# One barrier fewer, two steps earlier and a fed matrix engine at the joints of a graph network

## The reference

```
h = jnp.maximum(_layernorm(x, axis=-1), 0.0)
...
h = _gat_conv(x, src, dst, W1, att_src1, att_dst1, b1, N)
h = _leaky(_graph_norm(h, gn_weight, gn_bias, gn_mean_scale), NEG_SLOPE_ACT)
h = _gat_conv(h, src, dst, W2, att_src2, att_dst2, b2, N)
h = _graph_norm(h, gn_weight, gn_bias, gn_mean_scale)
return _leaky(h + residual, NEG_SLOPE_ACT)
...
out = jax.ops.segment_sum(x[col] * norm[:, None], row, num_segments=num_nodes)
```

## Time and profile before

| what | us |
| --- | --- |
| median of 3 runs (lowest, highest) | 862.6 (862.21, 863.18) |
| the profiled execution's own time | 864.48 |
| its span, from first to last instruction | 862.7 |
| mean granted clock of PE | 0.921 of full |
| PE busy, DVE busy, ACT busy | 747.3, 629.5, 478.8 |

### The profile page before, as it was taken

One profiled execution on the slowest core, in us unless ns is written; L12 is line 12 of the kernel. 1 busy time (PEld: TensorE's weight loads), 2 busy tenths in 40 slices (PEclk: granted clock), 3 DMA queues, 4 the chain that ended last, 5 costly groups with the idle time before them and its releaser, 6 DMA issues. The chain is left out here.

```text
span 862.7 us, 21079 instructions
## 1 busy us (share of the span) xinstructions
PE 747.3 (87%) x8209; PEld 680.8 (79%) x8209; DVE 629.5 (73%) x1696; ACT 478.8 (56%) x911; POOL 4.3 (0%) x14
## 2 busy tenths in 40 slices
PE   7898889887997998999997589988854999887898
PEld 6666656657996998999997578888753988876797
DVE  7899999985455544433444789998878999987732
ACT  2698889881004122122224588888665988874600
POOL 1000000000000000000000000000000000000000
PEclk9799999997997999999999579999955999998899
DMA  4000000005990000000002100000001489776901
GB/s 136 12 12 12 12 4 2 2 2 177 415 382 1 2 2 1 2 2 2 13 13 93 31 2 17 17 17 2 1 1 33 96 178 195 158 150 156 189 24 34
DMA packets 98735, 56.02 MB, mean 65 GB/s; under 512 B 91160, under 2 KB 93130, under 8 KB 98504
## 3 DMA queue, kind: packets, MB, share of 16 engines
q1 hardware_dynamic: 98292, 53.78, 23.0%
q10 hardware_dynamic: 340, 0.84, 0.3%
HBM read 9.16 MB, written 24.97 MB: 40 GB/s over the span
## 5 line engine op out<-in xcount | busy, mean ns | idle before, releaser
L631 PE MATMUL banks<-y_sb,adjacency 128*128 128x192 f16 (+1 forms) x1875 | 167.1, 250 | 6.0 <-DVE y_sb L668 5.2
L631 PEld LDWEIGHTS banks<-y_sb,adjacency 128*128 128x128 f16 x1875 | 162.6, 99 | 7.0 <-DVE y_sb L668 5.3
L469 PEld LDWEIGHTS counts<-hot_code,hot_row 128*128 128x128 f16 x1568 | 96.5, 103 | 59.9 <-DVE hot_code L352 35.4
L469 PE MATMUL counts<-hot_code,hot_row 128*128 128x100 f16 (+3 forms) x1568 | 124.8, 223 | 20.1 <-DVE hot_code L352 15.3
L1761 PE MATMUL banks<-loose,y_sb 128*128 128x194 f16 x540 | 101.4, 251 | 0.0
L352 DVE TENSOR_TENSOR hot_code<-codes_iota,unpacked 128x600 f16<-128x600 f16 x196 | 97.2, 563 | 0.0
L1760 PE MATMUL banks<-x_sb,gat_masks 128*128 128x194 f16 x420 | 79.8, 252 | 16.6 <-DVE gat_masks L1684 8.2
L572 ACT ACTIVATE adjacency<-counts 128x800 f16<-128x800 f32 x98 | 81.6, 833 | 21.5 <-PE counts L469 21.3
L1760 PE MATMUL banks<-x_sb,y_sb 128*128 128x194 f16 x400 | 75.0, 250 | 13.9 <-DVE h_sb L1684 9.9
L1731 ACT ACTIVATE gat_masks<-y_sb,node_scalars 128x640 bf16<-128x640 f32 x84 | 67.9, 825 | 23.1 <-PE banks L1761 17.9
L1760 PE MATMUL banks<-x_sb,h_sb 128*128 128x194 f16 x430 | 75.8, 247 | 0.8
(11 more groups left out here) (244 smaller groups left out, 1353.3 us busy)
## 6 DMA issues: line engine op xcount, KB each, us to landing
kept_adj<-adjacency SPq DMA_DIRECT2D x5, 4000.0 KB, 32.1
y_sb<-a_dst_rows SPq DMA_DIRECT2D x10, 320.0 KB, 3.5
window_keys<-edge_keys SPq DMA_DIRECT2D x188, 5.0 KB
residual<-h_sb SPq DMA_DIRECT2D x5, 240.0 KB, 2.0
kept_x<-x_sb SPq DMA_DIRECT2D x1, 1200.0 KB, 4.5
loose<-residual SPq DMA_DIRECT2D x5, 240.0 KB, 3.4
x_sb<-kept_x SPq DMA_DIRECT2D x5, 240.0 KB, 4.8
x_sb<-in_x SPq DMA_DIRECT2D x4, 240.0 KB
```

The source lines that it names most:

```text
L469: last = nc.tensor.matmul(counts[:, 2 * (p % HELD) + i, start:end], hot_row[:, q % 2, b * QUAD + w, :], hot_codes(q % 2, b)[:, w, start - ...
L631: return nc.tensor.matmul(k.ps[:, j % G, 0:cols], k.ADJ[:, i, j * P:(j + 1) * P], y[:, i, 0:cols], start=i == 0, stop=i == NT - 1)
```

## The change

Five edits. (1) The clearing of semaphores and the second meeting of all engines behind attention 1 are gone; a list of semaphores that are older than attention 1, without the two of `row_ready`, is cleared by POOL as its first instruction inside attention 1. (2) In both attentions piece 2 is measured ahead of the last five adds instead of behind `write`. (3) In graph_norm bn_aggr is issued ahead of three short instructions instead of behind them. (4) In `last_norm` `low(g - 1)` goes ahead of the lift in each round, and lifts 3 and 4 are both done in round 1. (5) In place of 48 idle-time matmuls in a row there are 83, in ten pieces, each behind a wait for a step of group 0 on DVE or ACT.

```diff
-def clear_semaphores(nc, k):
-    nc.clear_and_free_semaphores(k.held)
-    nc.all_engine_barrier()
-    k.held = []
...
+            measure(nc, k, dve, t.tiles_turned, t.measured, MEASURED_EARLY)
             for q in range(G):
                 add(NG - 1, q)
             write(NG - 1)
-            for n in range(MEASURED_EARLY, NC + 1):
+            for n in range(MEASURED_EARLY + 1, NC + 1):
                 measure(nc, k, dve, t.tiles_turned, t.measured, n)
...
         @block.gpsimd
         def _(pool):
+            if passed:
+                nc.clear_and_free_semaphores(passed)
...
+        chain.later(dve.bn_aggr(k.columns[:, 4:6], k.column_stats.rearrange("p n e -> p (n e)")))
         chain.later(dve.tensor_scalar(unit, k.mscale, -1.0, None, ALU.mult))
         chain(dve.tensor_scalar(less, k.mscale, -1.0, 1.0, ALU.mult, ALU.add))
-        chain.later(dve.tensor_tensor(less, less, k.gat_bias, ALU.mult))
-        chain(dve.bn_aggr(k.columns[:, 4:6], k.column_stats.rearrange("p n e -> p (n e)")))
+        chain(dve.tensor_tensor(less, less, k.gat_bias, ALU.mult))
...
             moments(g)
-            if g + 2 < NG:
-                lift(g + 2)
             if g >= 1:
                 low(g - 1)
+            for later in {0: (2,), 1: (3, 4)}.get(g, ()):
+                lift(later)
             scales(g)
...
-        keep_busy(sums(0)[:, 0:P], FILL_MORE)
+        for step, count, times in ((s.added, 1, 10), (s.measured, G, 14), (s.row_moments, G, 16), (s.row_shift, 1, 10)):
+            pe.wait_ge(step, count)
+            keep_busy(sums(0)[:, 0:P], times)
+        for t in range(G):
+            pe.wait_ge(s.normal, t + 1)
+            keep_busy(sums(0)[:, 0:P], 5)
+        pe.wait_ge(s.high, 1)
+        keep_busy(sums(0)[:, 0:P], 8)
         over_chunk(0, 0, AT_ONCE)
...
-        attend(nc, k, d, "gat1", d.gat_b1)
-        clear_semaphores(nc, k)
+        passed = [s for s in k.held if s not in k.row_ready]
+        attend(nc, k, d, "gat1", d.gat_b1, False, passed)
```

More of the change, by code:

```diff
@@ L1418, in turn_chunk, with attend @@
                      d.kept_adj[a * G * P:(a + 1) * G * P, m * G * P:(m + 1) * G * P], transpose=True).then_inc(k.adj_turned[m], 16)
-def attend(nc, k, d, name, b, last=False):
+def attend(nc, k, d, name, b, last=False, passed=()):
     with ExitStack() as c:
@@ L1880 @@
 LEAK = 0.01
-FILL, FILL_MORE = 32, 48
+FILL = 32
 def last_norm(nc, k, d, c, block):
```

## The result

Five executions of each in the first comparison: 862.6 us before (861.87 to 863.18), **857.1 us** after (856.79 to 858.68), ratio 0.9939 with a 95% interval of 0.9928 to 0.995. Two later comparisons of the same kernel gave 0.9941 (0.9922 to 0.9959) and 0.9938 (0.9921 to 0.9955). The forecast was 857.8 in a range of 856.3 to 860.0. The time was right, in part by luck: of the sum's terms 0.35 us was worth nothing and the largest had a cost beside it that the sum left out, while the clock in attention 2, which the sum had at nothing, gave about 1 us.

A forecast was written before the change was run, and what follows sets the result against it. The bound was the chain ending in PE's 54.64 us product, with DVE almost without pause ahead of it. Savings 1.29 + 0.60 + 0.35 + 0 + 0.37 + 2.2 = 4.8 us took 862.6 to 857.8, range 856.3 to 860.0.

The forecast's parts named there:

- Edit 1, 1.29 us: Behind attention 1: without the clearing, DVE's gap of 1.66 us falls to 0.37, saving 1.29 us.
- Edit 2, 0.60 + 0.35: Ends of both attentions: measuring piece 2 in DVE's idle time saves 0.60 us behind attention 1, 0.35 behind attention 2.
- from the last arrival to DVE's next instruction I keep 0.37: End of attention 2: norm 2 starts 0.37 us after SP, next late at 788.85, so 789.22 instead of 789.59.
- Edit 3, 0: Norms: issuing bn_aggr first saves nothing, as all four instructions are needed either way; between -0.1 and +0.1 us.
- Edit 4, 0.37: Ahead of the product: low of group 0 starts 0.37 us earlier, once ACT's float16 part ends; later group 1 work stays hidden.
- Edit 5, 2.2: Product: filler matmuls keep PE's clock up, so 29 steps at the lower clock go, saving 2.2 us.
- The last piece ends before the low part is done: Fillers ahead of the product: the last ends at 803.1, low of group 0 at 803.3, so no delay.
- rival (d): Ahead of the product: all 83 fillers run at the lower clock and start it 2.8 us late; 863.2 us, chance 0.03.
- The rise in attention 2, 0: Attention 2: the clock's rise moves with the work that starts earlier, so it adds nothing to the sum.
- rival (a): Attention 2: the rise stays put, giving back 0.95 us, 858.7; or comes earlier than its work, 857 or below; chance 0.22.
- the 5 us that the prediction named as a sign of being wrong: Attention 2: a clock rise more than 5 us after its dense matmuls begin would show the prediction wrong.
- The signs: Profile if right: DVE gap about 0.4 us, norm 2 0.3 to 0.4 after SP, clock 1.00 from transposes on, product 52.4 us.

The follow-up runs named there:

- the second execution: The changed kernel run again unaltered on a second chip: 858.25 us, ratio 0.9941 to the kernel before.
- The third: The changed kernel run a third time, unaltered, on a third chip: 857.26 us, ratio 0.9938 to the kernel before.

## Why the prediction held, point by point

- **Edit 1, 1.29 us:** right. The joint fell by 1.33 (1.66 to 0.33), and nothing came back at the head of attention 1, where PE's first mask matmul stands 4.71 us behind the last matmuls of the block ahead with the edit and without (492.37 to 497.08 in the changed kernel), nor behind norm 1 (-0.05 to attention 2). I had borrowed the price 0.37 from the joint behind attention 2, where SP and not DVE was the last; with DVE last it is 0.33. The two were near each other by accident.
- **Edit 2, 0.60 + 0.35:** the 0.60 behind attention 1 is what DVE's rows show. The 0.35 behind attention 2 was 0.03, so 0.3 of the sum was never there. The step that failed is "from the last arrival to DVE's next instruction I keep 0.37": SP had been the last arrival before the change as well, and a block starts about 0.73 us after SP's last issue, against 0.33 after DVE's last instruction. The joined loads showed it by taking SP out.
- **Edit 3, 0:** right within its bounds; the four instructions take 0.64 us instead of 0.69. It was not run alone.
- **Edit 4, 0.37:** right. The distance from the row variance (L690, at 802.35 before) to the low part of group 0 fell from 0.66 us to 0.28, and PE's wait alone by 0.37 (4.25 to 3.88). The later scales of group 1 held nobody up, and PE met no wait in the product.
- **Edit 5, 2.2:** the clock part is right, 2.3 us in the product, and the clock held through the holes. "The last piece ends before the low part is done" was wrong in the profiled execution: it takes for granted that the clock is up when the pieces begin. In the profile of before it came up at 794.95, ahead of them; after, it was up through the joint, fell at 789.1 and came back at 795.9, in their midst. Net gain there 2.28 - 0.79 = 1.5 us. That is the delay of rival (d) at a third of its size, without its lower clock in the product; of six profiles with the 83 matmuls two show it (0.8 and 0.7 us) and four don't. The price of (d) was also added up wrongly: the 2.8 us count from 803.4, and the sum beside it from the old start of 803.8, so it is 2.4 and 862.8 rather than 863.2.
- **The rise in attention 2, 0:** the step that failed is "my sum lets each rise move with its work". In this execution it moved with the work and more: 2.4 us after the dense matmuls began (656.97 to 659.4) instead of 4.2 (661.05 to 665.2; the 665.1 of the prediction is 0.1 early), and the attention took 1.2 us less, of which the rows explain the larger part: 1.8 us less at half speed is 0.9. That is rival (a)'s other side, the rise that comes earlier than its work. In the second execution it came 5.65 us after them (655.85 to 661.5), past the 5 us that the prediction named as a sign of being wrong. The Trainium skill's rule (TensorE: Matmul & The Clock Gate, "Part 1: The HAM clock gate"), by which the point of the rise depends on where the first matmul lands in a free-running window, fits what these executions of the same stretch show, 2.4 to 5.7 us; as a price for one execution it can't be forecast.
- **The signs:** as forecast are the joint behind attention 1, the measurement in the hole, the low part and the product in 52.4 us. Norm 2 came 0.72 us after SP's last issue, not 0.3 to 0.4, and the clock was not 1.00 from the transposes on but only from 795.9.
- **The sum, 4.8:** measured 5.5, 5.0 and 5.9 by medians. The joints and the product in the traces add up to 1.33 + 0.60 + 0.05 + 0.37 + 2.3, less 0 to 0.8 of delay: 3.9 to 4.7. The rest is the clock. From the first of the last adds of attention 1 to the last sum the first profile is 5.6 us shorter than before: 3.9 from those terms, 1.2 from attention 2, 0.5 from the 32 matmuls at the head of norm 2. The second has no delay (4.7) and the 0.5, but loses 0.4 in attention 2: 4.7. The third has no delay, 1.2 from attention 2 and 0.1 from norm 2: 6.0. So the forecast met the median because a missing 0.3 and a delay of 0 to 0.8 stood against about 1 us of clock in attention 2 and up to 0.5 in norm 2; that part is luck. The four edits alone sum to 3.9 by medians (1.75, 0.84, 1.62, and -0.31), each uncertain by about 1; none of the four profiles has a rise in attention 2 as early as those six. Why it came with all edits together in six profiles of seven, and how often it comes, was not tested and stays open.
- **The bounds:** the lower ends (0.6, 0.5, 0.2 and 1.9) sum to 3.2, which gives 859.4 and not 859.0; the stated range holds it all the same.

## What to carry to other kernels

At a meeting of all engines find the last arrival on every queue, SP's DMA issues included, before pricing a faster engine: here ten issues at about 0.43 us each made SP the last, and joining the loads was the cure. A matmul filler that keeps the clock up should fit its hole at the lower clock too, or it gives back part of what it was to save (0.8 of 2.3 us here). Where a stage begins with the lower clock and PE waits for its first operands, a few matmuls in that wait bring the rise forward; here that was worth 3.6 us by medians, more than the joints together. And a profile is compared by stretches, with the clock beside each: of two single profiles 7.7 us apart, 2.1 came from ahead of the change's first joint.

## What the runs showed of the hardware

- A block's start came 0.72 to 0.74 us after SP's last DMA issue in the kernel before, the changed one and all four single edits, 0.32 to 0.34 us after DVE's last instruction wherever DVE was last, and 1.66 us after it with the clearing and a second meeting between.
- One DMA issue of 1200 KB took SP 0.43 us in two profiles (1.10 and 1.45 in two others), five of 240 KB took 2.33.
- The clock's fall came after PE had resumed work in two executions (idle for 3.88 and 3.96 us, fall 1.2 us after the product's first matmul in both), so the first microseconds of a product can be fast and the next slow.
- The clock's rise in attention 2 came 3.9 to 7.3 us after PE's first mask matmul in seven profiles of kernels with the changed joints, 5.3 to 6.7 in five with the old ones or one edit, and 2.2 and 1.8 with 18 matmuls ahead of it.
- Executions of the kernel before spread from 860.58 to 865.77 us over 56 executions on three chips; terms of 0.4 to 0.7 us are seen in traces and not in medians of 5 to 12.
